# Sums of squares of two norms as products with a column of ones, in place of transposes and a VectorE sum, in a one-core recurrent and quantised block

## The reference, cut to what matters

```python
def rmsnorm(x, gamma):
    n = jnp.sqrt(jnp.sum(x * x, axis=-1, keepdims=True))
    return x / jnp.maximum(n, 1e-12) * x.shape[-1] ** 0.5 * (gamma + 1.0)
```

## Time and profile before

| | |
|---|---|
| median of 3 runs | 1067.97 us |
| the profiled execution: its time | 1067.32 us |
| the profiled execution: its span | 1065.5 us |
| PE busy | 1048.0 us, 98% of the span |
| PE weight loads busy | 970.0 us, 91% |
| DVE busy | 976.0 us, 92% |
| ACT busy | 627.4 us, 59% |
| POOL busy | 117.5 us, 11% |

### The profile page before, as it was taken

How to read it: one execution, slowest core, us unless ns; L and a number is a source line. 1 busy time by engine, 2 the same in 40 slices (tenths; PEclk the granted TensorE clock), 3 DMA queues, 4 the chain that set the end, 5 groups by cost and what they waited for, 6 DMA issues and landing times.

```text
span 1065.5 us, 18539 instructions
## 1 busy us (share of the span) xinstructions
PE 1048.0 (98%) x6924; PEld 970.0 (91%) x6924; DVE 976.0 (92%) x1883; ACT 627.4 (59%) x1010; POOL 117.5 (11%) x116
## 2 busy tenths in 40 slices
PE   7999999999999999999999999999999999999998
PEld 6788989999898999989999898999989899998998
DVE  7789999999999999999999999999999999999886
ACT  5675364574846557484565837456474655748452
POOL 1010102011020200102020010201102020010100
PEclk9999999999999999999999999999999999999999
DMA  7000001010010100001010010101001010100101
GB/s 252 1 20 2 1 21 41 21 40 2 22 40 21 41 20 19 23 21 41 21 41 21 1 41 21 41 21 41 14 8 40 21 41 21 39 3 1 41 1 60
DMA packets 29367, 31.47 MB, mean 30 GB/s; under 512 B 1120, under 2 KB 28512, under 8 KB 29280
## 3 DMA queue, kind: packets, MB, share of 16 engines
q1 hardware_dynamic: 28448, 29.43, 9.0%
q10 hardware_dynamic: 832, 0.87, 0.3%
HBM read 21.90 MB, written 8.39 MB: 28 GB/s over the span
## 4 chain that ended last, share of the span: by engine, by line
PE 67%; DVE 26%; ACT 3%; issue 3%; DMA 1%; POOL 0%; ACTq 0%; DVEq 0%
PE gu_ps L1065 35%; PE w_ps L1065 18%; DVE xs L575 3%; PE w_ps L1137 3%; DVE cand L573 2%; DVE cand L570 2%; DVE xs_lo L564 2%; DVE act_lo L527 2%; DVE q_y L411 2%; DVE hqt_lo L534 1%; DVE q_amax L399 1%; DVE hq L425 1%; ACT hqt_hi L858 1%; DVE hid L511 1%; PE gu_ps L1077 1%
## 5 line engine op out<-in xcount | busy, mean ns | idle before, releaser
L1065 PE MATMUL gu_ps<-gu_hi,xq_hi 128*128 128x352 f32 x512 | 167.8, 328 | 0.2 <-ACT act L888 0.2
L1065 PE MATMUL gu_ps<-gu_lo,xq_hi 128*128 128x352 f32 x512 | 165.7, 324 | 0.0
L1065 PE MATMUL gu_ps<-gu_hi,xq_lo 128*128 128x352 f32 x512 | 165.4, 323 | 0.0
L1065 PE MATMUL w_ps<-w_hi,act_hi 128*128 128x256 f32 x480 | 138.8, 289 | 0.8 <-DVE act_lo L527 0.8
L1065 PE MATMUL w_ps<-w_hi,act_lo 128*128 128x256 f32 x480 | 135.1, 282 | 0.0
L1065 PE MATMUL w_ps<-w_lo,act_hi 128*128 128x256 f32 x480 | 135.1, 281 | 0.0
L1065 PE MATMUL gu_ps<-xs_hi,w_hi 128*128 128x512 f32 x256 | 101.3, 396 | 0.0
L1065 PE MATMUL gu_ps<-xs_hi,w_lo 128*128 128x512 f32 x256 | 101.0, 394 | 0.0
L1065 PE MATMUL gu_ps<-xs_lo,w_hi 128*128 128x512 f32 x256 | 100.9, 394 | 0.0
L1065 PEld LDWEIGHTS gu_ps<-gu_hi,xq_hi 128*128 128x128 f32 x512 | 96.2, 188 | 0.5 <-issue 0.4
L1065 PEld LDWEIGHTS gu_ps<-gu_lo,xq_hi 128*128 128x128 f32 x512 | 96.3, 188 | 0.0
(11 more groups left out here) (156 smaller groups left out, 2710.0 us busy)
## 6 DMA issues: line engine op xcount, KB each, us to landing
x_in<-x_dram SPq DMA_DIRECT2D x16, 512.0 KB, 4.0
x_res<-x_dram SPq DMA_DIRECT2D x16, 512.0 KB, 4.8
out_dram<-o SPq DMA_DIRECT2D x15, 512.0 KB, 3.2
act<-w_t_dram SPq DMA_DIRECT2D x1, 1024.0 KB, 11.9
w_f<-w_t_dram SPq DMA_DIRECT2D x1, 1024.0 KB, 14.4
w_f<-w_down_dram SPq DMA_DIRECT2D x1, 704.0 KB, 9.9
hid<-w_gate_dram SPq DMA_DIRECT2D x1, 640.0 KB, 6.4
hid<-w_up_dram SPq DMA_DIRECT2D x1, 640.0 KB, 9.5
```

Of the source, the lines that this page charges most:

```text
L1065: done = M.matmul(psum, l, r, start=first and i == 0, stop=last and i == len(terms) - 1)
```

## The change

A column of 128 x 1 ones is set by POOL at the start. `sum_squares` multiplies each block of `sqs` (as before the stationary operand) with that column in place of the identity, by an ordinary matmul in place of a transpose, so that the sum over the partitions comes out of PE: 128 x 1 for each of the four blocks, side by side in the first four columns of the bank. DVE's reduction and the wait for its result go, and the scale and clamp read PSUM. PE's `sum_squares` gains a wait for the ones.

```diff
+        ones = sb("ones", [P, 1])
...
-        ss_sum = sb("ss_sum", [P, T])
...
+        ones_ready = sem("ones_ready")
...
         @block.gpsimd
         def _(pool):
             steps = Steps(pool_step)
+            nc.gpsimd.memset(ones[:], 1.0).then_inc(ones_ready, 1)
             constants = steps.mark(nc.gpsimd.memset(neg_half[:], -0.5))
             pool.wait_ge(pool_step, constants)
...
             def clamp_sums(n, bank):
 
                 dve.wait_ge(ss_done, n + 1)
-                s = steps.mark(V.tensor_reduce(ss_sum[:], bank.rearrange("p (t f) -> p t f", f=P), AX.X, ALU.add))
-                dve.wait_ge(dve_step, s)
-                V.tensor_scalar(ss_row[:], ss_sum[:], 1.0 / D, NORM_FLOOR_SQ / D, ALU.mult,
+                V.tensor_scalar(ss_row[:], bank[:, 0:T], 1.0 / D, NORM_FLOOR_SQ / D, ALU.mult,
                                 ALU.max).then_inc(ss_ready, 1)
...
             def sum_squares(n, bank, free):
 
+
+                pe.wait_ge(ones_ready, 1)
                 pe.wait_ge(sqs_ready, n + 1)
                 pe.wait_ge(*free)
                 for t in range(T):
-                    last = M.transpose(bank[:, t * P:(t + 1) * P], sqs[:, t * P:(t + 1) * P], ident[:])
+                    last = M.matmul(bank[:, t:t + 1], sqs[:, t * P:(t + 1) * P], ones[:], start=True, stop=True)
                 last.then_inc(ss_done, 1)
```

## The result

The changed kernel takes 1078.7 us (median of 4 runs, 1077.0 to 1079.38), against 1067.95 for the kernel before in the same count of runs: a ratio of 1.0099, 95% interval 1.0087 to 1.0111. It is slower, by 10.75 us where 14.1 were forecast. The profiled execution took 1077.0 us for a span of 1075.2, so 9.7 us more than before.

What follows compares the result with a forecast made beforehand. PE's instruction stream was taken to bound the kernel: 13.8 us for `body`'s sums plus 0.3 for the first chunk made +14.1, so 1082.0 us against the median. Own range 1080 to 1085 (63%), wider range 1076 to 1088 (81%).

Steps and rivals of the forecast that it cites:

- the price of a pair: At each sum on PE: eight load-bound pairs at 0.112 us, 0.90 us in place of 0.44, so +0.46 us.
- A: In PE's stream at the sum: columns set the pace, a sum costs 0.24 us, kernel faster at 1061; 6%.
- B: At PE's sums: loads as fast as a transpose's, +0.04 us a sum, no change at 1068.5; 6%.
- E: At PE's sums: no overlap of load and one-column product, +1.08 us a sum, so 1102; 5%.
- F: At PE's sums: four pairs for each product, not two, +1.35 us a sum, so 1111; 2%.
- DVE's relief: Dropping DVE's reductions, 22 us of its work, gains nothing in `body`; bound in favour 6.3 us.
- Rival C: Ahead of L534: pair price as forecast, but an earlier DVE ends the odd sum's 6.3 us wait: 1076; 9%.
- Rival D: At PE's sums: the extra wait for the ones costs up to 0.18 us each, 1082 to 1088; 9%.
- nothing to hide in: The 30 sums of `body` pay their added time in full in PE's stream: 30 x 0.46 = 13.8 us.
- the added wait: PE's wait for the ones, 32 times: costed at nothing, bounded at 5.8 us from L1186's loss of 0.18 each.
- the first chunk: The two sums of `first()`: +0.1 and +0.2 us, together +0.3 us.

Runs made afterwards that it cites:

- even_only: The change applied to the 16 even norms only, the odd ones as in the kernel before: 1074.86 us, ratio 1.0068.
- relief_only: Kernel before with its transposes, but without DVE's reduction; the clamp reads four columns of the bank, so norms are wrong: 1066.61 us, ratio 0.9991.
- plain_ident: Kernel before with its four transposes issued as plain float32 matmuls against the identity (128 columns), DVE's reduction kept: 1078.86 us, ratio 1.0106.
- sum3_as_before: Changed kernel with one sum of 32, that of norm 3, made as before: 1076.89 us, ratio 1.0093.
- f32r_sum2: Changed kernel with squares' sum and ones in float32r, two equal columns, DVE making the ones and PE waiting for them once: 1067.05 us, ratio 0.9999.

## Why the prediction was right or wrong

**Right: what bounds the kernel, the sign, and the price of a pair.** Eight pairs at 0.112 were the forecast for a sum; the even sum's +0.47, the +0.48 of even_only and the 1.79 for 16 pairs in the kernel with doubled products measure the same price three times. It goes with the pair and not with the columns: 128 columns in place of one change nothing, one pair in place of two changes everything. That it is the load in the pair that takes the 0.112 stays argued, since no run here has one-column matmuls without a load of their own. Rivals A, B, E and F, which had other prices for a sum, all fall with this. The Trainium skill, page "TensorE: Matmul & The Clock Gate", section "Back-to-back issue gap", gives about 60 cycles, or 25 ns, to a matmul of 1 to 64 columns by itself; the same section says that in a stream of loads and matmuls both set the spacing. The rows here bear out the second: 112 ns for a one-column matmul with a load of its own.

**Right: DVE's relief gives nothing in the chunks.** relief_only leaves the chunk at 63.01 us, and in the changed kernel the relief turns up as longer waits of DVE: ahead of L534, as forecast (22.2 us in all, 18.7 before), but more of it ahead of `scaled` (L558, 18.9 us, 2.6 before). Rival C falls: the loads' wait ahead of the odd sum is not shorter but a little longer, 7.0 us instead of 6.3. The distance from the load ahead to the sum's first grew from 0.54 us (515.38 to 515.92) to 0.59 (519.50 to 520.09), and it kept that length without the wait for the ones. Rival D, the price of that wait, falls too.

**Wrong: "nothing to hide in".** The failed step is the sentence that the 30 sums stand in PE's stream with nothing to hide in, and under it the reading that PE goes without a gap everywhere else in a chunk. The 15 odd sums had 0.31 us of waits behind them, and 15 x 0.31 = 4.7 us of the 13.8 went there. That leaves 9.1 for the chunks, and 9.7 came; the half microsecond between is not accounted for in full. The row was in front of me: the loads of L1186 waited 2.7 us in 14 times. I took its "issue" for a price of PE's queue and used it as a bound for the added wait, and so gave the one number that should have been subtracted a place where it could only be added. The other wait, for POOL, hung on the very reduction that the change removes, where I had written that PE never waits for DVE.

**Wrong, and small: the first chunk.** It was to cost 0.3 us and cost nothing (107.66 and 107.64 us at the even sum of chunk 1). Relief_only and plain_ident give the two sides of it: the reduction's end gives back 1.0 us there, the dearer sums take 1.1.

**Not foreseen: the clock.** It takes some 1.5 us in about half of the executions (4 of 8 of the changed kernel). So it moves the median up from the 1077.0 of the profiled execution, and towards the forecast for a reason that the forecast does not have.

**The range.** 1076 to 1088 holds the result, but the forecast's own, 1080 to 1085, does not; only the rivals C and D, which both proved false, had stretched it that far. That the result lies in it is luck.

## What to carry to other kernels

On PE, when the moving side is narrow, count load and matmul pairs and not columns: a plain float32 product against a single column costs two loads of the stationary tile and here twice the time of that tile's transpose, however little it computes; float32r makes it one, at the price of rounding the operands. Before giving work to the bounding engine to relieve another, find the instruction of the other that the bounding engine waits for, and judge the relief by that one alone. And a short pause marked "issue" is a wait until something else is shown: compare the start with the ends on the other engines, since a pause there is time that an added cost will fill first.

## What the runs showed of the hardware that I had not expected

- About half of the executions of the changed kernel have a granted clock of 0.998 (4 of 8), and the one that was profiled ran 3.4 us at 1.2 GHz, although PE had only stood for 1.2 us, then run 0.9 us of one-column pairs without pause and 1.3 us of ordinary products. With four transposes (sum3_as_before, even_only, relief_only, before) or with 128 columns (plain_ident) in the same place none of 64 runs does, nor with four float32r pairs (f32r_sum2) any of 11; with 16 one-column pairs a sum the clock fell four times in the profiled execution. The low stretch cost 1.5 us each time. What sets it off is not shown.
- The load of a transpose starts close behind that of a one-column product. The loads of the changed kernel around its odd sum:

```profile
519.50 0.19 PEld L1151 LDWEIGHTS w_ps<-dn_hi,hqt_hi 128*128 128x128 f32 x1
520.09 0.97 PEld L1123 LDWEIGHTS gu_ps<-ones,xs 128*128 128x128 f32 x8 [0.40 <-issue]
520.90 0.29 PEld L1188 LDWEIGHTS w_ps<-ident,x2b 128*128 128x128 f32 x2
```

The last of the eight starts at 520.09 + 0.97 - 0.19 = 520.87, and that of the transposes at 520.90, 0.03 later. With transposes (516.20 to 516.31) or 128 columns (522.27 to 522.38) in the sum it is 0.11, and so it is behind the changed kernel's even sums, where an ordinary load follows (492.31 to 492.42). It gives back about 0.08 us at each odd sum.
